# A graph network on one core: one product for both weight halves in two node stages, results taken by pairs of tiles

## The chip, the cores and the metric

The kernel runs on one NeuronCore of a Trainium2 chip. Its engines run side by side and meet at semaphores: TensorE (PE; its weight loads are listed as PEld), VectorE (DVE), ScalarE (ACT), GpSimd (POOL) and SyncE (SP, which here only issues transfers). The metric is the device time in microseconds (us) of one execution, as the median of several; lower is better.

## The reference

Four graph layers over 6250 nodes of 128 features and 100000 edges, each on the row-normalised x and with a residual sum: an attention layer, a convolution, an aggregation by mean, minimum, maximum and deviation (PNA), and a second attention layer (GATv2). What the two changed stages compute for the next layer, cut:

```python
h = jnp.maximum(_layernorm(x, axis=-1), 0.0)             # ahead of each layer
# PNA: the message of an edge, a product with both halves of W_pre
m = jnp.concatenate([h[dst], h[src]], axis=-1) @ W_pre + b_pre
...
# GATv2: two products of the same rows
x_l = x @ W_l + b_l
x_r = x @ W_r + b_r
h = x_l[src] + x_r[dst]
h = jnp.where(h >= 0, h, NEG_SLOPE * h)
e = h @ att
```

An edge's product is that of its two nodes, so both halves are computed by node: every node's row is multiplied by two weight matrices. That is what the changed lines do.

## The kernel before

The program alternates passes over the edges (hundreds of microseconds each) with short stages over the nodes. The 6250 nodes lie in 49 tiles of 128 rows. Two node stages matter here: the second one, `gcn_to_pna`, between the convolution and PNA, works by 13 chunks of four tiles; the last one, `pna_to_gatv2`, by 17 chunks of three (the last chunk has one tile). Both use the class `ResidualNorm`, whose object is `st`.

Each ends with the same software pipeline, written out by hand: every engine has a loop over turns j, and its order in a turn is the order of the code. Semaphores alone join the engines. In turn j of the last stage:

- ACT applies the column norm to chunk j (`apply`), normalises the rows of chunk j-2 (`normalise`, into `st.H`), and copies the turned chunk j-3 out of PSUM (`turned_in`, into `st.HT`, two buffers);
- PE turns chunk j back into rows (`back`, L804, into `st.TB`), turns the normalised chunk j-2 (`turn`, L860, into `st.TP`), and multiplies chunk j-3 by the weights W3 (L2676 and L2678, into `OP`);
- DVE adds chunk j to X (`add`, L813, which waits for `back`), computes row statistics (`statistics`, L820 and L824), finishes the row constants of chunk j-1 (`shift`, L836, which waits for POOL's root), and takes the products of chunk j-4 out of `OP`: L2751 adds a bias and writes the table rows T, L2753 writes XR and raises `st.taken`;
- SP stores T chunk by chunk as `st.taken` rises.

`OP` has four PSUM banks of 512 numbers. Before, a chunk uses two, one for each half of the weights, and the chunks alternate between two such sets, so that the products of chunk i wait until chunk i-2 was taken:

```python
wait(pe, st.taken, i - 1)
```

A wait for n is for the n-th rise of the semaphore; one for zero or less is left out. In the second stage `OP` holds a chunk's two halves in two banks, and again two chunks: ACT copies the first half into B (L2445, raising `b_in`), DVE adds b_pre to the second and writes PD (L2501). SP stores three arrays of every chunk: the turned rows, B and PD.

In the trace the tensors carry names: `f_OP` is `OP`, `r_TB`, `r_TP`, `r_H` and `r_HT` are those of `st`, `ACC` in L2751 is T, `XR3n` is XR, `f_B` and `f_PD` are B and PD. A float32 product of one instruction stands in the trace as two records, each with its own weight load; a float32 turn as one.

Of the kernel before, what the change touches and what calls it, by code (L numbers as in the profile page):

```python
# [15 lines left out]
ALU, ACT, AX = mybir.AluOpType, mybir.ActivationFunctionType, mybir.AxisListType  # L16

P = 128
D = 128
# [29 lines left out]
PNA_CP = 3  # L49
PNA_RING = 5  # L50
PNA_AHEAD = 2


def whole_program_tensors(nc, ctx):
# [647 lines left out]
class ResidualNorm:  # L702
# [54 lines left out]
    def width(self, j):  # L757
        return min((j + 1) * self.ch, TILES) - j * self.ch

    def cols(self, j):  # L760
        return slice(j * self.ch * P, min((j + 1) * self.ch, TILES) * P)

# [100 lines left out]
    def turned_in(self, act, j, out=None):  # L863

        act.wait_ge(self.turned, j + 1)
        if out is None:
            wait(act, self.product, j - 1)
            out = self.HT[:, j % 2, 0:self.width(j), :]
        self.nc.scalar.copy(out, self.TP[:, j % 2, 0:self.width(j) * P].rearrange("p (u n) -> p u n", n=P)).then_inc(self.ht_in, 1)

# [1505 lines left out]
def gcn_to_pna(nc, g, ACC):  # L2376

    with ExitStack() as ctx:
# [8 lines left out]
        PD = sb("PD", [P, TILES, D])  # L2387
        rs_in = sb("rs_in", [P, TILES])
        OP = ctx.enter_context(nc.psum_tensor("f1_OP", [P, 2, 2, 512], F32))
        counted = sem("counted")  # L2390
        rs_root = sem("rs_root")
        rows_scaled = sem("rows_scaled")
# [5 lines left out]
        with nc.Block() as block:  # L2398
# [28 lines left out]
            def _(act):  # L2427
# [7 lines left out]
                for j in range(st.n + 4):  # L2435
                    if j < st.n:
                        st.apply(act, j)
                    if 0 <= j - 2 < st.n:
                        st.normalise(act, j - 2)
                    if 0 <= j - 3 < st.n:  # L2440
                        st.turned_in(act, j - 3, HTF[:, st.tiles(j - 3), :])
                    i = j - 4
                    if i >= 0:
                        act.wait_ge(st.product, i + 1)
                        nc.scalar.copy(B[:, st.tiles(i), :], OP[:, i % 2, 0, 0:st.width(i) * D].rearrange("p (u d) -> p u d", d=D)).then_inc(b_in, 1)  # L2445

            @block.tensor
            def _(pe):
# [13 lines left out]
                for j in range(st.n + 3):  # L2462
# [5 lines left out]
                    if i >= 0:  # L2468
                        pe.wait_ge(st.ht_in, i + 1)
                        wait(pe, b_in, i - 1)  # L2470
                        wait(pe, st.taken, i - 1)
                        for half in range(2):
                            for u in range(st.width(i)):
                                ins = nc.tensor.matmul(OP[:, i % 2, half, u * D:(u + 1) * D], HTF[:, i * CH + u, :],
                                                       g["W2"][:, half * D:(half + 1) * D], start=True, stop=True)
                        ins.then_inc(st.product, 1)

            @block.vector
            def _(dve):
# [12 lines left out]
                for j in range(st.n + 4):  # L2492
# [4 lines left out]
                        st.shift(dve, j - 1)  # L2497
                    i = j - 4
                    if i >= 0:
                        dve.wait_ge(st.product, i + 1)  # L2500
                        V.tensor_tensor(PD[:, st.tiles(i), :], OP[:, i % 2, 1, 0:st.width(i) * D].rearrange("p (u d) -> p u d", d=D),  # L2501
                                        per_feature(g["b_pre"][:], st.width(i)), ALU.add).then_inc(st.taken, 1)
        sem.retire()

# [1 line left out]
def pna_to_gatv2(nc, g, ACC, XR, fin):  # L2506
# [5 lines left out]
    with ExitStack() as ctx:  # L2512
# [31 lines left out]
        u_turned = sem("u_turned")  # L2544
        stored = sem("stored")
        upto = [min((j + 1) * CP, TILES) for j in range(st.n)]

        with nc.Block() as block:
            @block.gpsimd
# [10 lines left out]
            def _(sp):  # L2560
# [8 lines left out]
                    sp.dma_start(HR[:, j % RING, 0:w * P], g["ht2"][:, st.cols(j)]).then_inc(hr_in[j % RING], 16)  # L2569
                rows = g["tab3"].rearrange("(t p) d -> p t d", p=P)  # L2570
                for j in range(st.n):
                    sp.wait_ge(st.taken, j + 1)
                    sp.dma_start(rows[:, st.tiles(j), :], T[:, st.tiles(j), :]).then_inc(stored, 16)
                sp.wait_ge(stored, 16 * st.n)

            @block.scalar
# [51 lines left out]
            def _(pe):  # L2628
# [37 lines left out]
                for j in range(st.n + 3):  # L2666
# [4 lines left out]
                    i = j - 3  # L2671
                    if i >= 0:
                        pe.wait_ge(st.ht_in, i + 1)
                        wait(pe, st.taken, i - 1)
                        for u in range(st.width(i)):
                            nc.tensor.matmul(OP[:, 2 * (i % 2), u * (D + 1):(u + 1) * (D + 1)], st.HT[:, i % 2, u, :],  # L2676
                                             g["W3"][:, 0:D + 1], start=True, stop=True)
                            ins = nc.tensor.matmul(OP[:, 2 * (i % 2) + 1, u * D:(u + 1) * D], st.HT[:, i % 2, u, :],  # L2678
                                                   g["W3"][:, D + 1:2 * D + 1], start=True, stop=True)
                        ins.then_inc(st.product, 1)  # L2680

            @block.vector
            def _(dve):
# [57 lines left out]
                for j in range(st.n + 4):  # L2741
# [3 lines left out]
                    if 0 <= j - 1 < st.n:  # L2745
                        st.shift(dve, j - 1)
                    i = j - 4
                    if i >= 0:
                        w = st.width(i)
                        dve.wait_ge(st.product, i + 1)  # L2750
                        V.tensor_tensor(T[:, st.tiles(i), :], OP[:, 2 * (i % 2), 0:w * (D + 1)].rearrange("p (u d) -> p u d", d=D + 1),  # L2751
                                        per_feature(g["b3"][:, 0:D + 1], w), ALU.add)
                        V.scalar_tensor_tensor(XR[:, st.tiles(i), :], OP[:, 2 * (i % 2) + 1, 0:w * D].rearrange("p (u d) -> p u d", d=D), -1.0,  # L2753
                                               per_feature(g["b3"][:, D + 1:2 * D + 1], w), ALU.mult, ALU.subtract).then_inc(st.taken, 1)
        sem.retire()


# [110 lines left out]
```

## Time and profile before

| what | value |
|---|---|
| device time, median of 3 runs | 4700.32 us (4696.98 to 4700.35) |
| the profiled execution | 4697.6 us, span 4695.4 us |
| mean granted TensorE clock | 0.738 of full speed |
| busy share of the span | PE 71%, POOL 70%, DVE 67%, ACT 52% |
| second node stage: first product to last store issued | 2260.8 to 2303.2 us |
| last node stage: first row turned back to last take | 3548.6 to 3597.7 us |

A row of a timeline is: start, duration, engine, line of the kernel, operation, out<-in, tile, number of like instructions merged (x3), and in brackets the idle time of the engine before it and what ended that. A table of stretches gives for each stretch its length and the busy time of PE, PEld, DVE, ACT and POOL, each with its number of instructions in brackets, then the granted clock (1.00 is 2.4 GHz, 0.50 is 1.2 GHz), the busy share of the DMA engines, and GB/s. Matmuls are pipelined, so the rows of PE overlap: what one costs is read from start to start.

### The profile page before, as it was taken

How to read it: one execution, taken by the hardware profiler on the slowest of the kernel's cores; microseconds unless marked ns; L12 is line 12 of the kernel's file. 1: busy time of each engine (PE TensorE's matmuls, PEld its weight loads, DVE VectorE, ACT ScalarE, POOL GpSimd, SP SyncE). 2: the span in 40 equal slices, each digit the busy share in tenths (PEclk: the TensorE clock that was granted, in tenths of full speed). 3: DMA queues.
4: the chain of work that ended last, by engine and by line, in shares of the span. 5: the costliest groups of instructions: out<-in, count | busy, mean ns of one | idle time of the engine just before them, and what ended most of it. 6: DMA issues, size and time to landing. Idle time of an engine off the chain costs nothing. (4 is left out here: it accounts for less than half of the span.)

```text
span 4695.4 us, 77185 instructions
## 1 busy us (share of the span) xinstructions
PE 3318.2 (71%) x21401; PEld 2878.4 (61%) x21401; DVE 3130.2 (67%) x8139; ACT 2442.2 (52%) x5474; POOL 3290.5 (70%) x3507
## 2 busy tenths in 40 slices
PE   4888888887533433344677777777796988888886
PEld 3666666666433333333576667667665877777776
DVE  5888888888533333333587777777666666766667
ACT  4776666664200000000787777777535666666665
POOL 4777777775677777776677777777524777777774
PEclk7555555556755666655799999999898888888887
DMA  7333333332122122221466666666523333333333
GB/s 139 89 88 88 88 88 87 89 88 47 53 53 53 53 53 53 53 53 46 130 191 179 188 186 188 184 182 187 155 63 75 80 82 82 80 81 81 82 80 76
DMA packets 368376, 468.65 MB, mean 100 GB/s; under 512 B 104163, under 2 KB 271331, under 8 KB 367968
## 3 DMA queue, kind: packets, MB, share of 16 engines
q0 software_dynamic: 107648, 226.35, 20.5%
q1 hardware_dynamic: 256208, 235.67, 16.7%
q8 instruction: 194, 3.18, 0.3%
q10 hardware_dynamic: 4112, 1.71, 0.1%
q14 instruction: 214, 1.75, 0.1%
HBM read 327.40 MB, written 134.06 MB: 98 GB/s over the span
## 5 line engine op out<-in xcount | busy, mean ns | idle before, releaser
L888 POOL DMA_INDIRECT e_G<-dr_tab,src_idx x832 | 792.4, 952 | 272.9 <-issue 232.8
L888 POOL DMA_INDIRECT m_G<-dr_tab,src_idx x832 | 785.3, 944 | 262.5 <-issue 203.2
L888 POOL DMA_INDIRECT v_G<-dr_tab,src_idx x832 | 791.1, 951 | 253.9 <-issue 247.5
L1838 POOL DMA_INDIRECT s_G<-dr_tab,chunk_src x784 | 739.9, 944 | 241.9 <-issue 237.4
L1922 PE MATMUL s_OUT<-s_G,s_S 128*128 x1664 | 378.3, 419 | 587.7 <-SPq L1865 556.4
L1922 PEld LDWEIGHTS s_OUT<-s_G,s_S 128*128 128x128 f32 x1664 | 352.9, 323 | 612.7 <-issue 612.7
L1877 DVE TENSOR_TENSOR ACC<-ACC,s_OUT 128x129 f32 x832 | 241.3, 290 | 623.8 <-PE s_OUT L1922 517.6
L2432 ACT COPY f_AT<-r_TP 128x512 f32<-128x512 f32 (+1 forms) x13 | 7.2, 554 | 973.2 <-PE r_TP L2454 973.2
L1316 PE MATMUL e_OUT<-e_RH,e_S 128*128 128x144 f32 x1664 | 511.3, 476 | 2.1 <-DVE e_RH L1202 2.1
L2149 DVE TENSOR_TENSOR ACC<-ACC,m_OUT 128x256 f32 x832 | 347.8, 418 | 236.0 <-PE m_OUT L2233 121.9
L1316 PEld LDWEIGHTS e_OUT<-e_RH,e_S 128*128 128x128 f32 x1664 | 404.6, 326 | 35.3 <-issue 21.6
L2232 PE MATMUL m_OUT<-m_G,m_S 128*128 128x128 f32 x1664 | 344.3, 290 | 55.4 <-DVE ACC L2149 54.8
L2107 ACT COPY m_XB<-m_BK 128x512 f32<-128x512 f32 x416 | 227.1, 588 | 231.5 <-PE m_BK L2216 229.4
L1657 DVE SCALAR_TENSOR_TENSOR ACC<-ACC,v_R,v_OUT 128x129 f32 x832 | 287.4, 345 | 86.3 <-DVE ACC L1657 3.1
L2233 PE MATMUL m_OUT<-m_SQ,m_S 128*128 128x128 f32 x1664 | 334.1, 284 | 0.0
L2232 PEld LDWEIGHTS m_OUT<-m_G,m_S 128*128 128x128 f32 x1664 | 268.2, 203 | 76.8 <-issue 74.2
L1228 DVE TENSOR_TENSOR ACC<-ACC,e_OUT 128x144 f32 x832 | 252.7, 304 | 88.2 <-DVE ACC L1228 2.7
L2207 PE MATMUL m_GT<-eye,m_G 128*128 128x128 f32 x832 | 131.9, 310 | 235.8 <-DMA m_G<-dr_tab,src_idx 188.0
L1748 PE MATMUL v_OUT<-v_RH,v_S 128*128 128x129 f32 x1664 | 287.6, 325 | 0.9 <-DVE ACC L1657 0.8
L1075 ACT ACTIVATE e_APART<-iota_row,e_LOC 128x128 bf16<-128x128 f32 x832 | 264.2, 388 | 3.4
L2233 PEld LDWEIGHTS m_OUT<-m_SQ,m_S 128*128 128x128 f32 x1664 | 265.9, 201 | 0.0
L1701 PE MATMUL v_NX<-v_ST,v_XR 128*128 128x128 bf16 x2496 | 253.9, 264 | 14.3 <-DVE v_others L1584 14.1
(381 smaller groups left out, 8028.0 us busy)
## 6 DMA issues: line engine op xcount, KB each, us to landing
dr_ends<-m_XB SPq DMA_DIRECT2D x416, 256.0 KB, 3.1
e_LR<-dr_row_loc SPq DMA_DIRECT2D x104, 256.0 KB
m_MS<-dr_row_start SPq DMA_DIRECT2D x104, 256.0 KB
v_LR<-dr_row_loc SPq DMA_DIRECT2D x104, 256.0 KB
e_G<-dr_tab,src_idx POOLq DMA_INDIRECT x832
m_G<-dr_tab,src_idx POOLq DMA_INDIRECT x832
v_G<-dr_tab,src_idx POOLq DMA_INDIRECT x832
s_G<-dr_tab,chunk_src POOLq DMA_INDIRECT x784, 2.5
```

What stands on the lines that cost most here:

```text
L888: pool.indirect_dma_start(out=out, out_offset=None, in_=table, in_offset=bass.IndirectOffsetOnAxis(ap=g["src_idx"][:, step:step + 1], axis ...
L1075: ins = nc.scalar.activation(APART[:, s, :], g["iota_row"][:], ACT.Square, bias=LOC[:, b, s:s + 1], scale=-1.0)
L1228: V.tensor_tensor(dst, dst, OUT[:, s // 3, (s % 3) * AC:(s % 3 + 1) * AC], ALU.add).then_inc(acc_done, 1)
L1316: nc.tensor.matmul(OUT[:, s // 3, (s % 3) * AC:(s % 3 + 1) * AC], S[:, b % 2, s, :], RH[:, b % 2, s, :], start=True, stop=True).then_inc(m ...
L1657: V.scalar_tensor_tensor(dst, dst, R[:, b % 2, s:s + 1], OUT[:, s // 3, (s % 3) * AC:(s % 3 + 1) * AC], ALU.mult, ALU.add).then_inc(acc_do ...
L1701: ins = nc.tensor.matmul(NX[:, s * P:(s + 1) * P], XR[:, bass.ds(tiles[step], 1), part, :].rearrange("p o d -> p (o d)"), ST[:, b % 2, ste ...
L1748: nc.tensor.matmul(OUT[:, s // 3, (s % 3) * AC:(s % 3 + 1) * AC], S[:, b % 2, s, :], RH[:, s, :], start=True, stop=True).then_inc(mm_done, 1)
L1838: pool.indirect_dma_start(out=G[:, c % (RING * GROUP), 0:D], out_offset=None, in_=table[:, :], in_offset=bass.IndirectOffsetOnAxis(ap=g["c ...
L1922: ins = nc.tensor.matmul(OUT[:, b, s // PER, (s % PER) * AC:(s % PER + 1) * AC], S[:, b, s, :], G[:, bass.ds(slot, 1), :].rearrange("p o c ...
L2149: V.tensor_tensor(dst, dst, OUT[:, q % 3, (s % 2) * 2 * D:(s % 2 + 1) * 2 * D], ALU.add).then_inc(acc_done, 1)
L2232: nc.tensor.matmul(OUT[:, q % 3, lo:lo + D], S[:, c, s, :], G[:, b, s, :], start=True, stop=True)
L2233: ins = nc.tensor.matmul(OUT[:, q % 3, lo + D:lo + 2 * D], S[:, c, s, :], SQ[:, c, s, :], start=True, stop=True)
```

## The change

Second stage: a tile's turned rows are multiplied by all 256 columns of W2 in one instruction (128 columns each in two before). A bank now holds two tiles with both halves each, so that ACT's half and DVE's half lie in the same bank; DVE's sum therefore waits for `b_in`, ACT's copy of the chunk, instead of for the product.

Last stage: a tile's rows are multiplied by all 257 columns of W3 in one instruction. The result fills one bank, so the four banks of `OP` hold four tiles. Products and takes go by pairs of tiles, counted through all 49: pair p lies in two banks and waits until pair p-2 was taken. A chunk has three tiles, so chunk 0 finishes one pair, chunk 1 two, chunk 2 one, and so on; `pairs_of(i)` are those finished with chunk i. A pair can hold the last tile of one chunk and the first of the next. `st.product` and `st.taken` count pairs, ACT's wait for a free `HT` is counted in pairs (`products_of`), and SP stores the pairs of a chunk in one transfer.

```diff
 # class ResidualNorm
+    def products_of(self, j):
+        return -(-min((j + 1) * self.ch, TILES) // PAIR) if j >= 0 else 0
+    def whole_pairs(self, j):
+        return self.products_of(j) if j >= self.n - 1 else max(0, (j + 1) * self.ch // PAIR)
...
-            wait(act, self.product, j - 1)
+            wait(act, self.product, self.products_of(j - 2))
...
 # gcn_to_pna
+        def product_rows(i, half):
+            return OP[:, i % 2].rearrange("p b (v m d) -> p (b v) m d", v=2, m=2)[:, 0:st.width(i), half, :]
...
-                        nc.scalar.copy(B[:, st.tiles(i), :], OP[:, i % 2, 0, 0:st.width(i) * D].rearrange("p (u d) -> p u d", d=D)).then_inc(b_in, 1)
+                        nc.scalar.copy(B[:, st.tiles(i), :], product_rows(i, 0)).then_inc(b_in, 1)
...
-                        for half in range(2):
-                            for u in range(st.width(i)):
-                                ins = nc.tensor.matmul(OP[:, i % 2, half, u * D:(u + 1) * D], HTF[:, i * CH + u, :],
-                                                       g["W2"][:, half * D:(half + 1) * D], start=True, stop=True)
+                        for u in range(st.width(i)):
+                            ins = nc.tensor.matmul(OP[:, i % 2, u // 2, (u % 2) * 2 * D:(u % 2 + 1) * 2 * D], HTF[:, i * CH + u, :],
+                                                   g["W2"][:], start=True, stop=True)
...
-                        dve.wait_ge(st.product, i + 1)
-                        V.tensor_tensor(PD[:, st.tiles(i), :], OP[:, i % 2, 1, 0:st.width(i) * D].rearrange("p (u d) -> p u d", d=D),
+                        dve.wait_ge(b_in, i + 1)
+                        V.tensor_tensor(PD[:, st.tiles(i), :], product_rows(i, 1),
...
 # pna_to_gatv2
+        W = 2 * D + 1
+        def pairs_of(j):
+            return range(st.whole_pairs(j - 1), st.whole_pairs(j)) if 0 <= j < st.n else range(0)
+        def pair_tiles(p):
+            return slice(p * PAIR, min((p + 1) * PAIR, TILES))
...
-                    sp.wait_ge(st.taken, j + 1)
-                    sp.dma_start(rows[:, st.tiles(j), :], T[:, st.tiles(j), :]).then_inc(stored, 16)
+                    tiles = slice(pair_tiles(pairs_of(j).start).start, pair_tiles(pairs_of(j).stop - 1).stop)
+                    sp.wait_ge(st.taken, pairs_of(j).stop)
+                    sp.dma_start(rows[:, tiles, :], T[:, tiles, :]).then_inc(stored, 16)
...
-                        wait(pe, st.taken, i - 1)
-                        for u in range(st.width(i)):
-                            nc.tensor.matmul(OP[:, 2 * (i % 2), u * (D + 1):(u + 1) * (D + 1)], st.HT[:, i % 2, u, :],
-                                             g["W3"][:, 0:D + 1], start=True, stop=True)
-                            ins = nc.tensor.matmul(OP[:, 2 * (i % 2) + 1, u * D:(u + 1) * D], st.HT[:, i % 2, u, :],
-                                                   g["W3"][:, D + 1:2 * D + 1], start=True, stop=True)
-                        ins.then_inc(st.product, 1)
+                        for p in pairs_of(i):
+                            wait(pe, st.taken, p - 1)
+                            tiles = pair_tiles(p)
+                            for t in range(tiles.start, tiles.stop):
+                                ins = nc.tensor.matmul(OP[:, t % 4, 0:W], st.HT[:, t // CP % 2, t % CP, :], g["W3"][:], start=True, stop=True)
+                            ins.then_inc(st.product, 1)
...
-                    if i >= 0:
-                        w = st.width(i)
-                        dve.wait_ge(st.product, i + 1)
-                        V.tensor_tensor(T[:, st.tiles(i), :], OP[:, 2 * (i % 2), 0:w * (D + 1)].rearrange("p (u d) -> p u d", d=D + 1),
-                                        per_feature(g["b3"][:, 0:D + 1], w), ALU.add)
...
+                    for p in pairs_of(i):
+                        tiles = pair_tiles(p)
+                        w = tiles.stop - tiles.start
+                        rows = OP[:, tiles.start % 4:tiles.start % 4 + w, 0:W]
+                        dve.wait_ge(st.product, p + 1)
+                        V.tensor_tensor(T[:, tiles, :], rows[:, :, 0:D + 1], per_feature(g["b3"][:, 0:D + 1], w), ALU.add)
+                        V.scalar_tensor_tensor(XR[:, tiles, :], rows[:, :, D + 1:W], -1.0,
+                                               per_feature(g["b3"][:, D + 1:W], w), ALU.mult, ALU.subtract).then_inc(st.taken, 1)
```

The order of PE's instructions in the last stage, kernel before, the turn in which chunk 2 is multiplied. The semaphores bear the names of their first holders: `e_own_done` is `ht_in`, `e_et_done` is `taken`, `e_beyond_done` is `h_done`, `e_r_done` is `applied`, `e_fac_done` is `x_in`.

```order
L804 MATMUL r_TB<-eye,r_UT 128x128 [waits e_fac_done,e_r_done]
L804 MATMUL r_TB<-eye,r_UT 128x128 x2
L860 MATMUL r_TP<-eye,r_H 128x128 [waits e_own_done,e_beyond_done]
L860 MATMUL r_TP<-eye,r_H 128x128 x2
L2676 MATMUL f_OP<-W,r_HT 128x129 [waits e_et_done,e_own_done]
L2678 MATMUL f_OP<-W,r_HT 128x128
L2676 MATMUL f_OP<-W,r_HT 128x129
L2678 MATMUL f_OP<-W,r_HT 128x128
L2676 MATMUL f_OP<-W,r_HT 128x129
L2678 MATMUL f_OP<-W,r_HT 128x128
```

PE in the changed kernel, from the one pair of chunk 2 through the two pairs of chunk 3 (L813 is `back`, L869 `turn`):

```order
L2698 MATMUL f_OP<-W,r_HT 128x257 [waits e_et_done,e_own_done]
L2698 MATMUL f_OP<-W,r_HT 128x257
L813 MATMUL r_TB<-eye,r_UT 128x128 [waits e_fac_done,e_r_done]
L813 MATMUL r_TB<-eye,r_UT 128x128 x2
L869 MATMUL r_TP<-eye,r_H 128x128 [waits e_own_done,e_beyond_done]
L869 MATMUL r_TP<-eye,r_H 128x128 x2
L2698 MATMUL f_OP<-W,r_HT 128x257 [waits e_et_done,e_own_done]
L2698 MATMUL f_OP<-W,r_HT 128x257
L2698 MATMUL f_OP<-W,r_HT 128x257 [waits e_et_done]
L2698 MATMUL f_OP<-W,r_HT 128x257
L813 MATMUL r_TB<-eye,r_UT 128x128 [waits e_fac_done,e_r_done]
L813 MATMUL r_TB<-eye,r_UT 128x128 x2
```

A turn has two or four products now instead of six, and every pair has a wait of its own for `taken`, ahead of the next `back`.

DVE in the last stage, kernel before, one turn (`e_factors_done` is `tb_done`, raised by `back`; `e_running_done` is `product`; `e_columns_done` is POOL's `root`; `e_drop_done` is `row_stats`):

```order
L813 TENSOR_TENSOR X<-r_TB,X 128x384 [waits e_factors_done]
L820 BN_STATS r_rs<-X 128x6 [waits e_fac_done]
L820 BN_STATS r_rs<-X 128x6 x2
L824 BN_AGGR r_mv<-r_rs 128x2 [waits e_drop_done]
L824 BN_AGGR r_mv<-r_rs 128x2 x2
L836 SCALAR_TENSOR_TENSOR r_nmr<-r_mv,r_rstd 128x3 [waits e_columns_done]
L2751 TENSOR_TENSOR ACC<-f_OP,b 128x3x129 [waits e_running_done]
L2753 SCALAR_TENSOR_TENSOR XR3n<-f_OP,b 128x384
```

DVE in the changed kernel, one turn that takes two pairs (the next takes one):

```order
L822 TENSOR_TENSOR X<-r_TB,X 128x384 [waits e_factors_done]
L829 BN_STATS r_rs<-X 128x6 [waits e_fac_done]
L829 BN_STATS r_rs<-X 128x6 x2
L833 BN_AGGR r_mv<-r_rs 128x2 [waits e_drop_done]
L833 BN_AGGR r_mv<-r_rs 128x2 x2
L845 SCALAR_TENSOR_TENSOR r_nmr<-r_mv,r_rstd 128x3 [waits e_columns_done]
L2772 TENSOR_TENSOR ACC<-f_OP,b 128x2x129 [waits e_running_done]
L2773 SCALAR_TENSOR_TENSOR XR3n<-f_OP,b 128x256
L2772 TENSOR_TENSOR ACC<-f_OP,b 128x2x129 [waits e_running_done]
L2773 SCALAR_TENSOR_TENSOR XR3n<-f_OP,b 128x256
```

The takes stay at the end of the turn, after `shift`, and are now two or four operations on two tiles instead of two on three.

## Rows read from the trace of the kernel before

**Rows 1.** The page, its head.

```profile
span 4695.4 us, 77185 instructions
```

**Rows 2.** Table of stretches: the sum pass, the last pass, the last node stage.

```profile
1500.00:2000.00 500.00, 195.13 (x852) 181.91 (x851) 182.73 (x477) 0.00 (x0) 377.81 (x402) 0.60 0.20 53
3800.00:4600.00 800.00, 704.97 (x5615) 624.84 (x5615) 558.22 (x1547) 499.38 (x1208) 604.77 (x640) 0.84 0.34 82
3562.00:3590.00 28.00, 24.19 (x193) 21.27 (x192) 26.05 (x108) 23.11 (x53) 10.69 (x22) 1.00 0.27 79
```

**Rows 3.** Timeline of DVE in the last node stage, two turns of its loop.

```profile
3569.42 0.56 DVE L813 TENSOR_TENSOR X<-r_TB,X 128x384 f32<-128x384 f32 x1 [0.24 <-PE r_TB L804]
...
3571.00 0.56 DVE L2751 TENSOR_TENSOR ACC<-f_OP,b 128x387 f32<-128x387 f32 x1
3571.47 0.55 DVE L2753 SCALAR_TENSOR_TENSOR XR3n<-f_OP,b 128x384 f32<-128x384 f32 x1
3571.93 0.55 DVE L813 TENSOR_TENSOR X<-r_TB,X 128x384 f32<-128x384 f32 x1
...
3574.77 0.56 DVE L813 TENSOR_TENSOR X<-r_TB,X 128x384 f32<-128x384 f32 x1 [0.25 <-PE r_TB L804]
```

**Rows 4.** Timeline of PE in the same stretch.

```profile
3568.89 0.49 PE L804 MATMUL r_TB<-eye,r_UT 128*128 128x128 f32 x3
3569.59 0.55 PE L860 MATMUL r_TP<-eye,r_H 128*128 128x128 f32 x3 [0.21 <-ACT r_H L847]
3569.98 0.46 PE L2676 MATMUL f_OP<-W,r_HT 128*128 128x129 f32 x2
3570.28 0.39 PE L2678 MATMUL f_OP<-W,r_HT 128*128 128x128 f32 x2
3570.50 0.39 PE L2676 MATMUL f_OP<-W,r_HT 128*128 128x129 f32 x2
...
3572.43 0.55 PE L860 MATMUL r_TP<-eye,r_H 128*128 128x128 f32 x3 [0.55 <-ACT r_H L847]
```

**Rows 5.** Timeline of DVE, the take of the last chunk, one tile.

```profile
3597.23 0.28 DVE L2751 TENSOR_TENSOR ACC<-f_OP,b 128x129 f32<-128x129 f32 x1
3597.43 0.28 DVE L2753 SCALAR_TENSOR_TENSOR XR3n<-f_OP,b 128x128 f32<-128x128 f32 x1
```

**Rows 6.** Timeline ahead of the last stage's loop: PE released by DVE.

```profile
3544.16 0.35 DVE L2719 SCALAR_TENSOR_TENSOR f_U<-f_OP,XR3n,f_T 128x128 f32<-128x128 f32 x1
...
3544.57 0.33 PE L2657 MATMUL r_TB<-eye,f_U 128*128 128x128 f32 x1 [0.98 <-DVE f_U L2719]
```

**Rows 7.** Timeline of PE ahead of that: eight records of 384 columns.

```profile
3537.49 2.75 PE L2647 MATMUL f_OP<-WF,f_HP 128*128 128x384 f32 x8
3540.07 0.38 PE L2649 MATMUL f_OP<-WF,f_HR 128*128 128x128 f32 x2
```

**Rows 8.** Timeline of PE at the start of the loop, at the lower clock.

```profile
3554.73 0.85 PE L804 MATMUL r_TB<-eye,r_UT 128*128 128x128 f32 x3
...
3556.48 0.64 PE L2676 MATMUL f_OP<-W,r_HT 128*128 128x129 f32 x2
3556.91 0.55 PE L2678 MATMUL f_OP<-W,r_HT 128*128 128x128 f32 x2
```

**Rows 9.** Table of stretches: second node stage, its middle and near its end.

```profile
2270.00:2280.00 10.00, 8.86 (x75) 8.01 (x74) 6.96 (x30) 9.73 (x21) 6.78 (x8) 1.00 0.71 238
...
2298.00:2300.00 2.00, 1.41 (x13) 1.22 (x11) 0.89 (x2) 0.75 (x2) 0.00 (x0) 1.00 0.98 313
```

**Rows 10.** Timeline of PE in the second node stage: one chunk's products.

```profile
2272.07 2.03 PE L2474 MATMUL f_OP<-W,f_HTF 128*128 128x128 f32 x16
2273.94 0.60 PE L804 MATMUL r_TB<-eye,r_UT 128*128 128x128 f32 x4
```

**Rows 11.** Timeline near the second stage's end: ACT's copy and DVE's sum.

```profile
2294.87 0.57 ACT L2445 COPY f_B<-f_OP 128x512 f32<-128x512 f32 x1
2294.88 0.68 DVE L2501 TENSOR_TENSOR f_PD<-f_OP,b_pre 128x512 f32<-128x512 f32 x1
```

More of the change, by code:

```diff
@@ L51 @@
 PNA_AHEAD = 2
+PAIR = 2
 def whole_program_tensors(nc, ctx):
@@ L2747, in _ @@
                     i = j - 4
-                    if i >= 0:
-                        w = st.width(i)
-                        dve.wait_ge(st.product, i + 1)
-                        V.tensor_tensor(T[:, st.tiles(i), :], OP[:, 2 * (i % 2), 0:w * (D + 1)].rearrange("p (u d) -> p u d", d=D + 1),
-                                        per_feature(g["b3"][:, 0:D + 1], w), ALU.add)
-                        V.scalar_tensor_tensor(XR[:, st.tiles(i), :], OP[:, 2 * (i % 2) + 1, 0:w * D].rearrange("p (u d) -> p u d", d=D), -1.0,
-                                               per_feature(g["b3"][:, D + 1:2 * D + 1], w), ALU.mult, ALU.subtract).then_inc(st.taken, 1)
+                    for p in pairs_of(i):
[6 more added lines that the diff above has]
+                                               per_feature(g["b3"][:, D + 1:W], w), ALU.mult, ALU.subtract).then_inc(st.taken, 1)
         sem.retire()
```

## The prediction

> **What bounds the kernel now.** The page is a mean over passes and node stages with different limits, and the change touches two short stages of the span [rows 1] alone, so I read those. I began with the table of stretches: in the last node stage, 3562 to 3590 us, DVE is busy for 26.05 of 28 us, PE for 24.19 and ACT for 23.11, at a granted clock of 1.00, which is 2.4 GHz [rows 2]. Then DVE's timeline of two turns of the loop: from one addition of L813 (3569.42) to the next but one (3574.77) it takes 5.35 us, 2.675 for a chunk of three tiles, and DVE waits for PE in one of the two turns, 0.24 us [rows 3]. So DVE bounds this stage, with PE close behind. PE's timeline shows the same loop from the other side: back into rows (L804), turn (L860), products (L2676, L2678), and short waits of 0.21 and 0.55 us for ACT [rows 4]. What the reader is to see: PE runs ahead of DVE. The products of a chunk are done before DVE comes to take them, and DVE's take of an older chunk is done before PE wants its banks again. Nobody waits for a take now.
>
> In the second node stage ACT is busy for 9.73 of 10 us in mid-stage, and in its last microseconds the DMA engines are at 0.98 of their time [rows 9]. PE bounds it in neither place.
>
> **The change part by part.**
>
> *Second stage, wider products.* A chunk's 16 records of 128 columns take from 2272.07 to 2273.94, 1.87 us, until the next work starts [rows 10]. Within a product two records are 0.22 us apart, while the first two take 0.30, so about 0.08 is start-up [rows 4]. Eight records of 384 columns take 2.58 us, 0.3225 each [rows 7]. Between 0.111 for 128 and 0.3225 for 384, one of 256 columns costs 0.217; eight make 1.73, with start-up 1.81. The gain is about 0.05 us a chunk: time goes with columns, and these stay. If all 13 chunks gave it to the end, 0.65 us.
>
> *Second stage, DVE's new wait.* DVE's sum (L2501) now waits for ACT's copy of the same chunk (L2445), and DVE's next addition is queued behind it. Late in the stage the two start together, 2294.87 and 2294.88, so the sum would start about 0.6 us later [rows 11]. What hides that is the store queue: the DMA engines are full there [rows 9]. If that cover is gone, 0.6 us at the end. The bounds of this stage are -0.65 and +0.6; I take 0, because ACT and the stores, which the change leaves alone, set its pace.
>
> *Last stage, what the pairs do to the order of waits.* This is the term that decides. Before, the products of chunk i waited for the take of chunk i-2, which DVE does one turn earlier. Now four banks hold four tiles, and pair p waits for the take of pair p-2. Chunks hold three tiles, so PE does alternately two pairs and one in a turn. Follow the numbers: chunk 1 has pairs 1 and 2, and pair 2 waits for pair 0; pair 0 belongs to chunk 0, which DVE takes in the very turn in which PE wants to start pair 2. Chunk 2 has pair 3, which waits for pair 1, taken first in DVE's same turn. So it goes on: in every turn one pair stands behind a take of the same turn. DVE's take comes after its addition, statistics and shift; and queued behind the waiting pair, on PE, is the next turn's L804, for which DVE's next addition waits. The two engines now work by turns:
>
> - addition's start to take's start: 3569.42 to 3571.00, 1.58 us [rows 3];
> - the take of a pair: the first operation lasts until the second starts, 0.47 us for three tiles [rows 3] and 0.20 for one [rows 5], so 0.335 for two; the second is 0.55 long for three and 0.28 for one, so 0.415;
> - DVE's end to PE's start: 3544.16 + 0.35 to 3544.57, 0.06 [rows 6];
> - four records of 257 columns at 0.217 and start-up 0.08: 0.95;
> - L804, 0.49, and 0.04 until DVE's addition (3568.89 + 0.49 to 3569.42) [rows 3, 4].
>
> The sum is 1.58 + 0.335 + 0.415 + 0.06 + 0.95 + 0.49 + 0.04 = 3.87 us for a turn where 2.675 stand now: 1.195 more. Turn (L860) and the other pair fit inside the 2.33 us in which DVE works; ACT's normalising too, with about 1 us to spare. The lock holds from the addition of chunk 4 to that of chunk 16, twelve intervals: 14.3 us. Ahead of it chunk 0 multiplies two tiles instead of three, which gives back about 0.4. Behind it, the last takes run as before. Net +13.9.
>
> The bounds of the untried piece, the two-tile take over two banks: as cheap as one tile (0.48, 0.27 less than 0.75) or as dear as three (1.02, 0.27 more), so 3.2 us either way over twelve turns; I take the middle, since two tiles lie halfway. The Trainium skill (Perfetto Trace Analysis, Optimizing Scalar/DVE Operations) puts the fixed part of a DVE instruction on PSUM at about 125 ns. The rows leave 65 ns (0.20 for 129 columns, 0.47 for 387), so they disagree with it; by the page a take would be 0.12 dearer and the sum 1.4 us larger, and I keep the rows.
>
> *Stores.* Still 17, of two or four tiles instead of three, behind the takes. They carry 79 GB/s at a DMA share of 0.27 [rows 2]: nothing.
>
> *Last stage, the clock.* PE's work in two turns stays what it is, 24.19/28 of 5.35 us or 4.6, but two turns now last 7.74: it would be busy for 60% of the time. Rows of other busy shares: the sum pass, 39% busy, was granted 0.60 of full speed; the last pass, 88%, 0.84; this stage today, 86%, 1.00 [rows 2]. So a falling clock is likely and its share uncertain. A turn at the lower level (1.2 GHz) costs: two records 0.43 apart instead of 0.217 [rows 8], so four add 0.85; L804 lasts 0.85 instead of 0.49; together 1.2. Bounds: none of the twelve turns, 0, or all, +14.4. On the line between 39% and 88% a share of 60% gives 0.70, which would be six turns; this stage's own row gives none. I take five, nearer the line because the present row has no PE gaps over 0.6 us and the new loop has waits of 0.8 to 1.7: +6.0. The Trainium skill (TensorE: Matmul & The Clock Gate, A second HAM failure mode) tells of a kernel that cycled through PSUM banks, idled briefly between groups of products, and swung between the two levels. By that the +6.0 belongs in the sum; by this stage's own row it would be +13.9 alone.
>
> **The rivals.**
>
> *The clock holds.* The same lock at 1.00 throughout: 4700.3 + 13.9 = 4714. For it: this stage's own clock. Against it: the two passes above.
>
> *The clock stays low for the whole stage:* 13.9 + 14.4, 4729. For it: 0.60 in the sum pass. Against it: 0.60 is a mean of both levels too, at a lower busy share than the new loop's.
>
> *Not slower: the take comes early enough.* If DVE took pair p-2 before PE got to pair p, the wait would cost nothing and the stage would stay DVE's; its takes would grow by 0.13 in two turns (three pairs at 0.75 less the overlap of 0.08, against two of 0.935), about 1 us in all, less the second stage's gain: 4701. It decides at PE's arrival: about 0.6 us after the addition's start in turns with one pair, 1.5 in turns with two, against a take that ends 2.33 after. It is short by 1.7 and 0.8, and today's gaps of 0.24 to 0.55 don't cover that. It holds only if I have put pairs into the wrong turns.
>
> *Faster: weight loads were the brake.* Half of them go, 98 records in each stage. But two products start 0.22 apart, close to what their columns take at any width, so loads are hidden; and DVE's own work (2.51 of 2.675 us) would let at most 2 us through, ACT's in the other stage about as much: 4696, still within 0.2%. Only something outside these stages makes it faster by more.
>
> **How the numbers follow.** On the profiled execution: span 4695.4 [rows 1] + 13.9 + 6.0 + 0 = 4715.3. That execution took 4697.6, 2.2 over its span; the median shown is 4700.32, 4.9 over the span. So the median of the changed kernel is forecast at 4715.3 + 4.9 = 4720. Chances: this forecast 0.52; clock holds 0.26; low throughout 0.08; not slower 0.12; faster 0.02. The range runs from 4709 (clock holds and the takes are cheap) to 4728 (nearly all turns low); it leaves out the last two cases and most of the third, with tails of the others, some 2 in 10. A measurement of this kernel tells about 0.2%, 9.4 us, from no change. The cases above that hold 0.86; 0.02 of it falls back below the bound, so slower 0.84, same 0.14, faster 0.02.
>
> **What would show it.** In the last stage: DVE additions 3.87 us apart, 5.1 where the clock is low, instead of 2.51 and 2.84; DVE waiting for L804's successor in every turn, 1.5 us in turns with one pair and 0.9 with two; PE idle ahead of a pair with DVE's second take as releaser; granted clock below 1.00 in part. The whole stage 20 us longer, the second one equal within 0.7. Wrong: intervals near 2.7 (pairs in other turns than I think), or intervals of 3.87 and a clock of 1.00 (then 4714).

## The result and the profile after

| what | before | after |
|---|---|---|
| device time, median of 9 runs each | 4699.34 us | 4714.05 us (4709.6 to 4716.01) |
| ratio to before, 95% interval | | 1.003 (1.0022 to 1.0039) |
| span of the profiled execution | 4695.4 us | 4712.6 us |
| second stage: first addition to the last PD store's issue | 51.21 us | 50.65 us |
| last stage: first addition to the end of the last take | 48.19 us | 64.07 us |

One of the nine executions before took 5120.92 us, the other eight 4694.87 to 4701.37, and the ratio leaves that one out. The change makes the kernel slower, by 14.7 us of the medians where 19.7 were forecast. The loss sits in the last node stage, 15.9 us longer, while the second gains 0.6; the rest of the 17.2 between the two spans lies in passes that the change doesn't touch: the second stage began 2.62 us later, the stretch from it to the last stage was 2.84 shorter, the pass behind that 2.12 longer, and 2.62 - 0.56 - 2.84 + 15.88 + 2.12 = 17.2. Such shifts say nothing of the change, so the stages below are compared by their own traces.

The same stretches of the table as in [rows 2], after (length; PE, PEld, DVE, ACT, POOL busy with counts; clock; DMA share; GB/s):

```profile
1500.00:2000.00 500.00, 195.54 (x853) 182.43 (x853) 182.74 (x477) 0.00 (x0) 377.78 (x402) 0.60 0.20 53
3562.00:3590.00 28.00, 17.07 (x85) 13.41 (x86) 18.59 (x79) 15.64 (x35) 7.32 (x14) 0.94 0.17 50
```

The sum pass is as it was. In the last node stage every engine has become idler: DVE 26.05 to 18.59 of 28 us, PE 24.19 to 17.07, ACT 23.11 to 15.64. No engine bounds it any more, which is what a chain of engines waiting for each other looks like. DVE's timeline after, against [rows 3], a turn that takes one pair and one that takes two:

```profile
3565.30 0.56 DVE L822 TENSOR_TENSOR X<-r_TB,X 128x384 f32<-128x384 f32 x1 [0.95 <-PE r_TB L813]
...
3566.89 0.42 DVE L2772 TENSOR_TENSOR ACC<-f_OP,b 128x258 f32<-128x258 f32 x1
3567.22 0.42 DVE L2773 SCALAR_TENSOR_TENSOR XR3n<-f_OP,b 128x256 f32<-128x256 f32 x1
3569.19 0.56 DVE L822 TENSOR_TENSOR X<-r_TB,X 128x384 f32<-128x384 f32 x1 [1.55 <-PE r_TB L813]
...
3570.77 0.42 DVE L2772 TENSOR_TENSOR ACC<-f_OP,b 128x258 f32<-128x258 f32 x1
3571.11 0.42 DVE L2773 SCALAR_TENSOR_TENSOR XR3n<-f_OP,b 128x256 f32<-128x256 f32 x1
3571.44 0.42 DVE L2772 TENSOR_TENSOR ACC<-f_OP,b 128x258 f32<-128x258 f32 x1
3571.77 0.41 DVE L2773 SCALAR_TENSOR_TENSOR XR3n<-f_OP,b 128x256 f32<-128x256 f32 x1
3573.14 0.56 DVE L822 TENSOR_TENSOR X<-r_TB,X 128x384 f32<-128x384 f32 x1 [0.95 <-PE r_TB L813]
```

PE's timeline of the same turns, against [rows 4]:

```profile
3563.83 1.10 PE L2698 MATMUL f_OP<-W,r_HT 128*128 128x257 f32 x4 [2.19 <-DVE XR3n L2773]
3564.78 0.49 PE L813 MATMUL r_TB<-eye,r_UT 128*128 128x128 f32 x3
3565.10 0.49 PE L869 MATMUL r_TP<-eye,r_H 128*128 128x128 f32 x3
3565.43 1.03 PE L2698 MATMUL f_OP<-W,r_HT 128*128 128x257 f32 x4
3567.69 1.14 PE L2698 MATMUL f_OP<-W,r_HT 128*128 128x257 f32 x4 [1.23 <-DVE XR3n L2773]
3568.66 0.49 PE L813 MATMUL r_TB<-eye,r_UT 128*128 128x128 f32 x3
...
3571.67 1.10 PE L2698 MATMUL f_OP<-W,r_HT 128*128 128x257 f32 x4 [2.19 <-DVE XR3n L2773]
```

The circle can be read off. DVE's take ends (3567.22 + 0.42 = 3567.64), PE starts the pair that waited for it (3567.69), then the next chunk's `back` (3568.66), then DVE adds (3569.19). DVE's waits name PE and PE's name DVE: each engine stands while the other works. An addition came every 2.675 us before; now the intervals are 3.89 and 3.95.

The clock fell twice in this stage, in two turns in the middle and again from its last turn on. Four stretches of the table after: ahead of the first fall, in it, behind it, and in the second; then PE in the first, against [rows 8]:

```profile
3555.00:3579.00 24.00, 14.55 (x75) 11.22 (x75) 15.98 (x72) 14.60 (x33) 6.47 (x13) 0.97 0.13 39
3579.00:3584.00 5.00, 4.43 (x15) 3.29 (x16) 3.28 (x14) 2.83 (x8) 1.63 (x3) 0.66 0.18 53
3584.00:3606.00 22.00, 12.97 (x68) 10.28 (x69) 14.21 (x61) 11.76 (x29) 5.54 (x12) 0.96 0.19 55
...
3603.00:3608.00 5.00, 4.53 (x15) 3.79 (x16) 3.24 (x12) 3.13 (x9) 1.57 (x3) 0.66 0.27 79
```

```profile
3579.50 1.25 PE L2698 MATMUL f_OP<-W,r_HT 128*128 128x257 f32 x4 [2.19 <-DVE XR3n L2773]
3580.55 0.85 PE L813 MATMUL r_TB<-eye,r_UT 128*128 128x128 f32 x3
```

Second stage, PE's product of one chunk, against [rows 10]; then, near the stage's end, one of DVE's sums before and two with the new wait after, against [rows 11]:

```profile
2271.47 1.97 PE L2486 MATMUL f_OP<-W,f_HTF 128*128 128x256 f32 x8
2273.27 0.60 PE L813 MATMUL r_TB<-eye,r_UT 128*128 128x128 f32 x4
```

```profile
2297.10 0.69 DVE L2501 TENSOR_TENSOR f_PD<-f_OP,b_pre 128x512 f32<-128x512 f32 x1 [1.54 <-PE f_OP L2474]
```

```profile
2297.89 0.69 DVE L2513 TENSOR_TENSOR f_PD<-f_OP,b_pre 128x512 f32<-128x512 f32 x1 [0.52 <-ACT f_B L2458]
2300.08 0.69 DVE L2513 TENSOR_TENSOR f_PD<-f_OP,b_pre 128x512 f32<-128x512 f32 x1 [1.50 <-ACT f_B L2458]
```

A chunk's products take 1.80 us instead of 1.87, and the sum does wait for ACT's copy. But 0.52 and 1.50 are not what the new wait costs, for near the end the sum waited before as well, 1.54 us, for the product: counted from the stage's first addition, the sum of 2300.08 starts 45.47 us in, that of 2297.10 before 45.11, so 0.36 later.

### The profile page after: what moved, and what is told of

It reads as the page before. It is cut to its first block and busy times, and to the rows that moved or that the text cites. A ratio compares the mean times of both kernels' runs of the same rounds, so it can differ in the third digit from the quotient of the medians.

```text
span 4712.6 us, 76809 instructions
## 1 busy us (share of the span) xinstructions
PE 3322.5 (71%) x21205; PEld 2871.9 (61%) x21205; DVE 3131.9 (66%) x8155; ACT 2442.7 (52%) x5474; POOL 3293.6 (70%) x3507
## 5 line engine op out<-in xcount | busy, mean ns | idle before, releaser
L1540 ACT COPY v_NXS<-v_NX 128x512 f32<-128x512 f32 x208 | 120.5, 579 | 275.1 <-PE v_NX L1710 272.1
```

## The experiments

Theory: the pairs turn a wait for a take of the turn before into a wait for a take of the same turn, so that PE and DVE stand while the other works. Rivals: the wide product itself, the dearer take, or the clock makes the difference. "The twelve turns" are those from the addition of chunk 4 to that of chunk 16: 31.87 us before, 47.57 after.

### One half of the change each

Second stage alone (the kernel before, with `gcn_to_pna` of the changed kernel):

> The second stage of the changed kernel, the last stage of the kernel before. My theory (the whole cost lies in the last stage's order of waits): the time of the kernel before, 4699 us within its noise; additions in the last stage 2.5 and 2.8 us apart; the second stage from its first addition to its last store issue within 0.7 us of the 51.2 us that it takes before. Rival (the wide products and DVE's later sum in the second stage carry a part): 2 us or more longer in that stage.

Last stage alone (the changed kernel, with `gcn_to_pna` of before):

> The last stage of the changed kernel, the second stage of the kernel before. My theory: the time of the changed kernel, 4714 us, 14 to 17 over the kernel before on the same chip, with additions 3.9 us apart in the last stage. Rival (second stage carries a part): less than that, by what the other half costs.

| kernel | median | before, beside it | ratio (95%) | second stage | twelve turns |
|---|---|---|---|---|---|
| second only | 4698.89 | 4699.03 | 0.9997 (0.9987 to 1.0007) | 50.87 | 31.88 |
| last only | 4716.77 | 4699.03 | 1.0037 (1.0023 to 1.0051) | 51.11 | 49.31 |

The whole loss belongs to the last stage. The second stage gains a few tenths that a total can't show; over all the runs of this study, it lasts 51.05 to 51.35 us with narrow products and 50.22 to 51.02 with wide ones.

### The order of the takes and of `back`

Takes first: DVE's block of takes moves ahead of its addition.

```diff
                 for j in range(st.n + 4):
                     i = j - 4
+                    for p in pairs_of(i):
...
                     if j < st.n:
                         st.add(dve, j)
                         st.statistics(dve, j)
                     if 0 <= j - 1 < st.n:
                         st.shift(dve, j - 1)
-                    for p in pairs_of(i):
```

> The changed kernel, but DVE takes the pairs of a turn ahead of its addition instead of behind the row constants. Wide products, pairs, banks and the wait's count stay. My theory (a pair waits for a take of the same turn, and that take comes late in the turn): walking the waits with the measured durations, the interval between additions falls from 3.9 to about 3.1 us, since the addition now stands behind the take, and the stage is about 9 us shorter: 4705. Rival (the operations themselves are dearer: two-bank takes, eight more DVE instructions, wide records): nothing changes, 4714.

The median is 4705.68 against 4699.03, ratio 1.0013 (1.0003 to 1.0022); the twelve turns take 38.30 us. DVE's, ACT's and PE's timelines, takes first:

```profile
3571.65 0.13 DVE L845 SCALAR_TENSOR_TENSOR r_nmr<-r_mv,r_rstd 128x3 f32<-128x3 f32 x1
3572.42 0.43 DVE L2767 TENSOR_TENSOR ACC<-f_OP,b 128x258 f32<-128x258 f32 x1 [0.64 <-PE f_OP L2698]
```

```profile
3569.57 1.26 ACT L856 ACTIVATE r_H<-X,r_nmr,r_rstd 128x128 f32<-128x128 f32 x3 [1.61 <-DVE r_nmr L845]
```

```profile
3570.89 0.55 PE L869 MATMUL r_TP<-eye,r_H 128*128 128x128 f32 x3 [1.87 <-ACT r_H L856]
3571.27 1.98 PE L2698 MATMUL f_OP<-W,r_HT 128*128 128x257 f32 x8
```

PE no longer waits for a take, but DVE now waits for products that stand behind ACT's normalising, which stands behind DVE's own `shift`. Of the 15.7 us of loss in the twelve turns 9.3 are gone. A longer, weaker circle over three engines holds most of the rest, with intervals of 2.24 and 3.84; two intervals of 5.19 and 5.05, in which products and `back` lasted longer at the lower clock, hold 2.6 of it.

`back` one turn ahead, on PE alone:

```diff
+                st.back(pe, 0)
                 for j in range(st.n + 3):
-                    if j < st.n:
-                        st.back(pe, j)
+                    if j + 1 < st.n:
+                        st.back(pe, j + 1)
```

> The changed kernel, but PE turns a chunk back into rows (L813) one turn earlier, so that the next addition's input does not stand behind the waiting pair. The wait and the takes stay as they are. My theory (the wait costs because the next L813 is queued behind it): intervals of about 2.7 us, as in the kernel before, the last stage some 16 us shorter than in the changed kernel: 4698. Rival (the pair's late take holds the loop by itself, whatever stands behind it): intervals stay at 3.9, 4714. Rival (dearer operations): the same.

The median is 4698.19 against 4699.03, ratio 0.9998 (0.9989 to 1.0008): the loss is gone. The twelve turns take 31.63 us. The table and DVE's timeline, `back` ahead:

```profile
3562.00:3588.00 26.00, 22.36 (x124) 17.01 (x123) 25.31 (x112) 22.79 (x53) 10.59 (x21) 1.00 0.27 77
```

```profile
3567.33 0.55 DVE L822 TENSOR_TENSOR X<-r_TB,X 128x384 f32<-128x384 f32 x1
...
3569.57 0.55 DVE L822 TENSOR_TENSOR X<-r_TB,X 128x384 f32<-128x384 f32 x1
...
3572.47 0.55 DVE L822 TENSOR_TENSOR X<-r_TB,X 128x384 f32<-128x384 f32 x1
```

PE's timeline, `back` ahead:

```profile
3568.61 0.55 PE L813 MATMUL r_TB<-eye,r_UT 128*128 128x128 f32 x3 [0.38 <-ACT r_UT L803]
3568.99 0.49 PE L869 MATMUL r_TP<-eye,r_H 128*128 128x128 f32 x3
3569.32 1.90 PE L2699 MATMUL f_OP<-W,r_HT 128*128 128x257 f32 x8
```

The pairs, the wide products, the takes and the waits for them are those of the changed kernel. Only the instruction queued behind the waiting pair is no longer the one for which DVE waits. DVE is busy for 25.31 of 26 us, without a wait: it bounds the stage again, at intervals of 2.24 and 2.90. The waits for the takes stand in the code, but PE no longer stands at them: its short idle time, 0.38 us, is now for ACT's column norm, and the takes come in time.

### Is it the width, or the length of the take?

Pairs with narrow products (a tile's columns 0 to 128 and 129 to 256 as two instructions, all else as changed):

> The changed kernel, but in the last stage each tile is multiplied by the two halves of the weights in two products again (129 and 128 columns); pairs, banks, waits and takes stay. My theory (width gives nothing, the order of waits costs): eight records at 0.111 us instead of four at 0.217, so a locked turn is about 0.02 us longer, 3.9 to 4.0 between additions; the stage within 3 us of the 64 that the changed kernel shows, the clock deciding the rest. Rival (the wide product is what slows the stage): intervals fall towards 2.7.

A single execution took 4713.06 us against 4705.21; its intervals are 3.91 and 3.97, 0.02 over the wide product's. So the width is not the brake; the lock is that of the pairs and their waits.

A longer take (a third operation, which copies columns into an unused part of T's buffer, ahead of the release):

```diff
                                                per_feature(g["b3"][:, D + 1:W], w), ALU.mult, ALU.subtract)
+                        V.tensor_tensor(ACC[:, tiles, D + 1:2 * D], rows[:, :, 0:D - 1], per_feature(g["b3"][:, 0:D - 1], w), ALU.add)
```

> The changed kernel with a third operation in each take: it copies 127 columns a tile of the pair once more from PSUM into unused columns, ahead of the release of the banks. My theory (the first take of a turn lies in the lock, the second beside PE's work): about 0.33 us more in every turn, 4.2 to 4.3 instead of 3.9, some 4 us for the stage, and more of it at the lower clock, because PE is busy for a smaller share. Rival (DVE's total work sets the pace): 0.33 more in turns with one pair, 0.66 in turns with two.

DVE's timeline, longer take:

```profile
3567.36 0.41 DVE L2773 SCALAR_TENSOR_TENSOR XR3n<-f_OP,b 128x256 f32<-128x256 f32 x1
3567.69 0.41 DVE L2775 TENSOR_TENSOR ACC<-f_OP,b 128x254 f32<-128x254 f32 x1
3569.78 0.56 DVE L822 TENSOR_TENSOR X<-r_TB,X 128x384 f32<-128x384 f32 x1 [1.69 <-PE r_TB L813]
...
3574.06 0.56 DVE L822 TENSOR_TENSOR X<-r_TB,X 128x384 f32<-128x384 f32 x1 [0.62 <-PE r_TB L813]
```

The operation adds 0.33, and the intervals at the higher clock grow from 3.89 and 3.95 to 4.22 and 4.28: by 0.33 in every turn, those with two pairs too, where DVE does the operation twice and its wait shrinks. One take per turn lies in the circle and the other does not, as the theory's sum has it. (A single execution, 4719.16 us against 4705.21.)

### The lock without pairs, and the clock

The kernel before, whose chunk waits for the chunk just before it:

```diff
-                        wait(pe, st.taken, i - 1)
+                        wait(pe, st.taken, i)
```

> The kernel before, but the products of chunk i wait for the take of chunk i-1 instead of i-2: one semaphore count more, no pairs, no wide products. DVE takes chunk i-1 in the same turn. My theory (a wait for a take of the same turn locks PE and DVE): the interval is the sum of the parts, 1.58 to the take, 0.47 and 0.55 for the take of three tiles, 0.06, products 1.41, L804 0.49, 0.04: 4.6 us instead of 2.675, for 12 or 13 turns, so 23 to 27 us more, 4723 or above with turns at the lower clock. Rival (pairs or wide products are needed for the loss): 4699.

The median is 4749.25 against 4705.21, ratio 1.0092 (1.0077 to 1.0108). The same circle appears without pairs or wide products, but the twelve turns take 71.33 us, 5.9 each: the expected price of 4.6 was missed by the clock. To tell the clock from the lock, the same kernel with PE's idle time filled (`turn` is done six times over, `st.turn(pe, j - 2, 6)`):

> The kernel of e6_old_lock (products wait for the take of the chunk before), but PE turns every normalised chunk six times over instead of once, in the time in which it waits: 15 more records of 0.107 us, no other work. My theory (of the 45 us that e6_old_lock loses in the stage about half is the lock, the rest the lower clock that PE's idle time brings): the granted clock stays at 1.00, the interval is 4.6 to 4.7 us, the stage about 73 us instead of 93, the whole some 25 us over the kernel before instead of 44. Rival (the low clock is incidental or has another cause): clock near 0.6 again and the stage at 93 us or longer by the added work.

The median is 4733.67 against 4702.72, ratio 1.0066 (1.005 to 1.0081). The table and PE's wait, first without the fill, then with it:

```profile
3565.00:3625.00 60.00, 37.73 (x179) 34.53 (x178) 25.32 (x100) 22.12 (x50) 10.46 (x20) 0.61 0.12 34
```

```profile
3568.24 0.77 PE L2676 MATMUL f_OP<-W,r_HT 128*128 128x129 f32 x2 [2.15 <-DVE XR3n L2753]
```

```profile
3562.00:3622.00 60.00, 50.13 (x430) 47.44 (x428) 32.65 (x128) 28.25 (x65) 13.35 (x26) 1.00 0.15 44
```

```profile
3578.74 0.46 PE L2676 MATMUL f_OP<-W,r_HT 128*128 128x129 f32 x2 [0.82 <-DVE XR3n L2753]
```

Filled, the clock is 1.00 and the interval 4.69, near the 4.6 worked out; the twelve turns take 56.04 us. So of the 39.5 us which they lost without the fill, 24.2 are the lock and 15.3 the clock, since PE still waits for the take with the fill (0.82 us) and the added turns lie in its idle time. The whole stage takes 80.36 us, more than expected, because its ends lose as well: 12.27 us from the first addition to that of chunk 4 (9.21 before) and 12.05 behind that of chunk 16 (7.11 before).

The changed kernel, filled alike (`st.turn(pe, j - 2, 4)`):

> The changed kernel with every normalised chunk of the last stage turned four times instead of once, in the time in which PE waits for a take (nine more records of 0.107 us). My theory: clock 1.00 throughout the loop, no interval over 4.0, the stage 63 us or a little less (64.1 in the changed kernel's trace, 66.8 in that of e2_last_only, which spent more time at the lower clock). Rival: low turns as before, or all turns longer by the added work.

```profile
3562.00:3606.00 44.00, 35.53 (x237) 30.18 (x237) 29.16 (x123) 24.48 (x56) 11.54 (x22) 1.00 0.17 49
```

That is the table's row, filled: 1.00 throughout, and the twelve turns take 47.05 us against 47.57 in the changed kernel's execution and 49.31 in that of the last stage alone, whose row follows, with a clock of 0.88:

```profile
3560.00:3609.00 49.00, 31.55 (x142) 24.34 (x142) 30.95 (x132) 26.29 (x60) 12.59 (x24) 0.88 0.16 44
```

So the clock cost 0.5 us of the twelve turns in the one and 2.3 in the other. In the one it lengthened two intervals, 4.40 where others like it take 3.95 and the last, 4.05 where the filled kernel has 3.73; that is 0.8, and the filled kernel's first interval of 4.14 takes part of it back. In the other, PE's rows show a turn whose waiting pair and `back` both ran at the lower clock:

```profile
3598.65 2.05 PE L2695 MATMUL f_OP<-W,r_HT 128*128 128x257 f32 x4 [2.19 <-DVE XR3n L2770]
3600.49 0.85 PE L813 MATMUL r_TB<-eye,r_UT 128*128 128x128 f32 x3
```

The pair takes 1.84 us instead of 0.95, and the interval is 5.21 instead of 3.89. As a repair the fill is worthless: it costs 1.5 us at the start and 0.9 at the end, so that the stage lasts 65.94 us, more than the 63 expected and the 64.07 without it (a single execution, 4719.77 against 4702.72).

### Is there more to gain?

`back` ahead with the narrow last stage of before and the wide second stage:

> The second stage of the changed kernel, and the last stage of the kernel before with L804 one turn earlier on PE. Walking the waits: intervals of 2.5 to 2.6 us instead of 2.675, DVE's own work (2.51) as the bound; the stage 2 to 3 us shorter than the 48.2 of the kernel before, so 4696 to 4697, which a measurement of the whole can hardly tell from 4699. Rival (the change's pairs are needed for that, since they free banks sooner): 48.2 us in the stage.

The same, and `back` ahead in the second stage too:

> The kernel of e8_old_back_ahead, and in the second node stage too PE turns a chunk back into rows one turn earlier. Aimed at a version that beats both kernels. My theory: in the second stage a product no longer stands ahead of the next L804, ACT's own work (3.2 us a chunk against a mean interval of 3.4) becomes the bound, and the stage is 1 to 2 us shorter than 50.6, unless its stores, which fill the DMA engines at the end, set it: then 0. With the 1 us of the last stage 2 to 3 us below the kernel before, ratio 0.9994. Rival (stores set the stage): ratio 0.9998.

| kernel | median | before, beside it | ratio (95%) | second stage | twelve turns |
|---|---|---|---|---|---|
| last stage's `back` ahead | 4703.6 | 4705.21 | 0.9995 (0.9986 to 1.0005) | 50.40 | 31.41 |
| both | 4706.26 | 4702.72 | 1.0009 (0.9999 to 1.0018) | 58.68 | 31.18 |

Neither beats the kernel before by an amount that can be told. In the last stage DVE's waits of 0.24 go and the intervals are 2.51, but the first of the twelve grows from 2.52 to 3.84 and 3.61, so that only 0.5 to 0.7 us of the twelve turns are gained; the whole stage is 47.29 us in the first kernel, 0.9 shorter and not 2 to 3. In the second stage the same edit costs 8 us, against the 1 to 2 of gain expected. PE's and ACT's timelines there, both ahead:

```profile
2280.12 0.66 PE L804 MATMUL r_TB<-eye,r_UT 128*128 128x128 f32 x4 [1.39 <-ACT r_UT L794]
2280.61 0.60 PE L860 MATMUL r_TP<-eye,r_H 128*128 128x128 f32 x4
2281.05 1.89 PE L2478 MATMUL f_OP<-W,f_HTF 128*128 128x256 f32 x8
2284.32 0.66 PE L804 MATMUL r_TB<-eye,r_UT 128*128 128x128 f32 x4 [1.39 <-ACT r_UT L794]
```

```profile
2282.97 0.58 ACT L2449 COPY f_B<-f_OP 128x512 f32<-128x512 f32 x1 [0.91 <-PE f_OP L2478]
2283.46 0.81 ACT L794 ACTIVATE r_UT<-r_UT,r_shf,r_scl 128x512 f32<-128x512 f32 x1
```

Here ACT takes products itself, and its column norm for the next `back` (L794) is queued behind that copy. With `back` ahead, PE waits for ACT in the turn in which ACT waits for PE: another circle, 4.20 us a turn (2280.12 to 2284.32) where the changed kernel alternates between 3.21 and 3.53.

## Why the prediction was right

**The lock: right, term by term.** The turn with one pair was forecast at 3.87 and measures 3.89. Its terms after, with the forecast behind each: addition to take 1.59 (1.58); the take's first operation 0.33 (0.335) and its second 0.42 (0.415); DVE to PE 0.05 (0.06); four records 0.97 (0.95); `back` to addition 0.53 (0.49 + 0.04). Turns with two pairs take 3.95, since PE starts 0.14 behind the take there (3571.11 + 0.42 to 3571.67) instead of 0.05. DVE's waits of 1.55 and 0.95 are the 1.5 and 0.9 forecast, and PE waits for DVE's second take, as said. So the twelve intervals cost 15.2 without the clock (47.05 less 31.87) where 14.3 were forecast. That one wait makes this, and that the order of the queued work sets its price, is shown by four runs: `back` ahead removes it, the longer take adds its 0.33, narrow products change nothing, and chunks of three tiles lock alike once they wait for the chunk just before.

**The two-tile take: the middle was right.** 0.75 was chosen between 0.48 and 1.02. The Trainium skill (Perfetto Trace Analysis, Optimizing Scalar/DVE Operations) would have made it, by an estimate from its 125 ns of fixed part on PSUM, 0.12 dearer; the take of 0.33 + 0.42 disagrees with that, and the rows' 65 ns stand.

**PE's waits: 2.19 and 1.23 where 1.7 and 0.8 were forecast.** The short wait for ACT's `H` that [rows 4] show ahead of `turn` is gone, because in the longer turn ACT is done in time; so PE reaches the waiting pair earlier. That costs nothing.

**Start and tail: -0.5 and +0.65.** The first was forecast at -0.4: the interval ahead of chunk 4 fell from 3.11 to 2.64, and from 4.23 to 3.47 between the two kernels with one half of the change, so its sign is right and its size differs between executions. The tail, from the addition of chunk 16 to the last take, was put at nothing; it grew from 7.11 to 7.76. The pairs don't make this: with narrow pairs, whose tail ran at 1.00, it is 7.19, and with `back` ahead 7.11. In the changed kernel's execution the clock was 0.66 there, so most of the 0.65 belongs to the clock.

**The second stage: 0 forecast, some -0.5 measured** (the mean of eight executions with wide products against four with narrow ones). It lies inside the bounds of -0.65 and +0.6. The product cost 1.80 us where 1.81 was worked out. Near the end a sum starts 0.36 later in the stage than before, where 0.6 was forecast; the stage got shorter all the same, so that this was covered.

**The clock: the step that failed.** Five of twelve turns at the lower level were put in at 1.2 each, +6.0. Measured is +0.5 in the twelve turns and most of the tail's 0.65, and in another execution of the same last stage +2.3 in the twelve turns. The price of a turn was near: 1.3 where the waiting pair and `back` both ran low (5.21 instead of 3.89). The number of such turns was not. And a low turn doesn't always cost: in the turn behind the one of 4.40, PE's products ran low in part, but its wait of 1.23 went instead, and the interval stayed 3.89. The number was chosen on a line through stretches of different busy share, and the changed stage refutes this line: PE is busy for 61% (17.07 of 28) and 64% (31.55 of 49) at 0.94 and 0.88, where the line gives about 0.7. The old lock is busy for 63% (37.73 of 60) at 0.61, but that share is not a like one, since the same work lasts longer at the lower clock (`back` 0.85 instead of 0.49 us). What decides where the clock falls is not settled here. Shown is only that, in these two kernels, work put into PE's idle time kept it at 1.00. The Trainium skill (TensorE: Matmul & The Clock Gate, A second HAM failure mode) warns of a clock that swings when PE cycles through PSUM banks and idles briefly between groups; the changed kernel agrees in kind, with 0.66 in two stretches of 5 us, but hardly in price.

The rival "the clock holds", 4714, thus came nearer than the forecast of 4720, which kept its sign and its range; the clock's term accounts for most of the 6 us between. The range's lower end of 4709 is not what its terms give (4714.2 - 3.2 = 4711), but nothing hangs on that here. By this execution's own terms the sum is 15.2 + 0.5 - 0.5 + 0.65 = 15.9 in the last stage and -0.6 in the second: 15.3, against 14.7 between the medians.

## What to carry to other kernels

Where buffers are counted anew (by pairs instead of chunks), recount how many turns lie between a result and the wait that frees its place: below one full turn, two engines that ran side by side work by turns, and no operation has to get dearer for it. Then look at what is queued behind the waiting instruction: moving the one that the other engine needs ahead of it, here `back` on PE, undid a loss of 15 us, while the same move in a stage where ACT takes the products made a new circle. Price a wait by its circle from the trace's rows, and the clock by a range.

## What the runs showed of the hardware

The clock cost more than half of what the wait itself cost (15.3 beside 24.2 us in the old lock). Turns repeated for nothing (L860, six times) held it at 1.00, as the run's theory had it, and made that kernel 13 us faster than without them (31.0 over its runs of before instead of 44.0). And a float32 product of 257 columns costs what two of 129 and 128 into the same bank cost: intervals of 3.89 against 3.91 us.
